# Scores of two heads at once on four quarters of TensorE, in two attention layers of a decoder kernel

## What is computed

```python
q_hk = (hidden_q @ Wq.T).reshape(Bv, Sv, H, K)
q_big = jnp.einsum('bshk,hkq->bshq', q_hk, w_kc_q)
q_big = _apply_rope(q_big, sin_q[None, :, None, :], cos_q[None, :, None, :])
kv_r = _apply_rope(kv_c, sin_k[None], cos_k[None])
q_r = jnp.einsum('bshq,hqr->bhsr', q_big, W_qr)
k_r = jnp.einsum('bld,hdr->bhlr', kv_r, W_kr)
scores = jnp.einsum('bhsr,bhlr->bhsl', q_r, k_r)
attn = jax.nn.softmax(scores, axis=-1)
ctx_c = jnp.einsum('bhsl,bld->bhsd', attn, kv_r)
ctx_lat = jnp.einsum('bhsd,hkd->bhsk', ctx_c, w_kc_kv)
```

## Time and profile before

| | us |
|---|---|
| runs, median (lowest, highest) | 1348.82 (1344.62, 1350.92) |
| profiled execution, its own time | 1344.42 |
| its span, first to last instruction | 1342.7 |
| TensorE busy in it | 1245.0 |
| VectorE busy | 798.1 |
| ScalarE busy | 591.1 |
| second layer's attention loop, first to last scores | 435.07 to 490.32 |
| third layer's attention loop, first to last scores | 829.69 to 961.60 |

### The profile page before, as it was taken

The page is one execution under the profiler, slowest core; times in us unless marked ns, Lnnn a source line. Parts: engine busy times, 40 slices in busy tenths (PEclk is TensorE's granted clock), DMA queues, the critical chain, the costliest instruction groups (busy, mean ns, idle before and its releaser), DMA issues. The chain is left out here.

```text
span 1342.7 us, 30256 instructions
## 1 busy us (share of the span) xinstructions
PE 1245.0 (93%) x12658; PEld 932.8 (69%) x12658; DVE 798.1 (59%) x1511; ACT 591.1 (44%) x1070; POOL 378.9 (28%) x323
## 2 busy tenths in 40 slices
PE   6999998989999999999999889999997888999988
PEld 3479994559977677788867667888774445676545
DVE  5764566863363764633358665888644775873762
ACT  3632334684554674433433431232532453662751
POOL 0164303046630000555520005544102043532100
PEclk9999999999999999999999999999998999999999
DMA  4000004046024001000075080000016421211000
GB/s 125 4 2 4 4 4 127 1 109 131 1 68 146 2 2 36 1 0 1 1 165 166 1 264 1 1 1 2 2 71 199 133 61 47 55 30 33 2 1 32
DMA packets 81047, 68.36 MB, mean 51 GB/s; under 512 B 24968, under 2 KB 76880, under 8 KB 80784
## 3 DMA queue, kind: packets, MB, share of 16 engines
q1 hardware_dynamic: 78096, 63.63, 16.8%
q0 software_dynamic: 768, 2.10, 0.5%
q10 hardware_dynamic: 2048, 0.70, 0.2%
HBM read 53.82 MB, written 8.39 MB: 46 GB/s over the span
## 5 line engine op out<-in xcount | busy, mean ns | idle before, releaser
L1955 PE MATMUL ps<-rounded 128*128 128x512 f32 x384 | 91.2, 393 | 2.0 <-POOL rounded L1988 1.0
L1688 PE MATMUL ps<-fixed 128*128 128x512 bf16 x361 | 89.6, 389 | 1.9 <-PEq L78 1.9
L1342 POOL TENSOR_TENSOR fixed<-fixed,cross 128x768 f32<-128x768 f32 x32 | 58.9, 1839 | 104.5 <-DVE cross L1291 104.5
L1955 PEld LDWEIGHTS ps<-rounded 128*128 128x128 f32 x384 | 70.9, 188 | 20.3 <-POOL rounded L1988 5.3
L1256 PE MATMUL ps<-rounded 128*128 128x256 f32 x576 | 76.8, 287 | 1.3 <-DVE cross L1287 1.3
L1256 PEld LDWEIGHTS ps<-rounded 128*128 128x128 f32 x576 | 70.7, 190 | 5.4 <-issue 3.2
L1988 POOL TENSOR_TENSOR rounded<-weights,rounded 128x256 fp32r<-128x256 f32 x32 | 23.6, 760 | 179.7 <-ACT rounded L2006 179.7
L1321 ACT COPY cross<-ps 128x256 f32<-128x256 f32 x32 | 11.9, 372 | 112.9 <-PE ps L1265 112.9
L1688 PEld LDWEIGHTS ps<-fixed 128*128 128x128 bf16 x361 | 34.7, 99 | 37.8 <-issue 6.9
L2095 DVE TENSOR_TENSOR work<-work,ps 128x512 f32<-128x512 f32 x32 | 22.0, 687 | 62.0 <-ACT work L2023 59.9
L1629 POOL TENSOR_TENSOR work<-weights,work 64x512 f32<-64x512 f32 x32 | 41.2, 1287 | 54.3 <-DMA work<-work 33.5
(11 more groups left out here) (497 smaller groups left out, 3056.0 us busy)
## 6 DMA issues: line engine op xcount, KB each, us to landing
weights<-in_L_ffn_masksT SPq DMA_DIRECT2D x32, 256.0 KB, 6.1
weights<-in_L_ffn_fc_w SPq DMA_DIRECT2D x16, 256.0 KB
weights<-in_L_xattn_Wq SPq DMA_DIRECT2D x2, 2048.0 KB, 10.1
weights<-in_L_xattn_WoT SPq DMA_DIRECT2D x2, 2048.0 KB, 11.1
work<-work SPq DMA_DIRECT2D x64, 64.0 KB, 2.0
sorted_in<-work SPq DMA_DIRECT2D x1, 3072.0 KB, 15.3
work<-sorted_in SPq DMA_DIRECT2D x12, 256.0 KB, 2.9
sorted_out<-work SPq DMA_DIRECT2D x12, 256.0 KB, 2.1
```

The costliest lines, as they stand in the source:

```text
L1342: nc.gpsimd.tensor_tensor(ro[:, v % 2, :, :], ro[:, v % 2, :, :], sn, ALU.add).then_inc(s["roped"], 1)
L1688: k.nc.tensor.matmul(k.ps[:, bank, :], k.ident16, k.causal, start=True, stop=True)
L1955: last = nc.tensor.matmul(ps[:, 2 * (n % 2) + i, :], a[:, q % 2, i, c, :], b[:, c, half * BANK:(half + 1) * BANK], start=c == 0 and part = ...
```

## The change

In both layers the scores of two heads are made together (`pair_scores`), in every second iteration: 32 matmuls that go round all four quarters, head e of the pair into bank 4 + e. They wait until both former heads' scores are subtracted. In the second layer head e takes the row half e, sequence b the column half b % 2. In the third layer the row half is b % 2 and the column half (b + e) % 2, so that a bank gets results from both row halves; `qb` is laid out anew for that, and the second head's probabilities have their partition halves exchanged, which `weigh` undoes in its access pattern.

In the third layer ("halved") also:
- `narrow` uses the quarters for the first two of its three parts (8 matmuls of 64 x 64 x 128, the zero blocks are left out) and two column halves for the third (4 matmuls of 128 x 64 x 128), into the first 128 columns of the banks 2 and 3.
- A turn goes to the upper 256 columns of banks 2 and 3 in place of a bank of its own; turns wait for the copy of the narrow product, narrow products for the copy of a turn.
- TensorE's order in an iteration becomes: project 2h, narrow 2h - 1, tiles 0 and 1 of project 2h + 1, turn, tile 2 of it, scores (of a pair, in every second iteration), narrow 2h, weigh.
- ScalarE does the hook "act_b" (copy of narrow 2h, rounding of weights) after the copy of the turned block.

VectorE's and GpSimd's programs are unchanged. The diff's core:

```diff
+        def pair_scores(h):
+            if h >= 2:
+                pe.wait_ge(s["centred"], h)
+            pe.wait_ge(s["q_ready"], q_hooks["ready"](h))
+            for b in range(BATCH):
+                tok, at = b * SEQ, (b // 2) * SEQ
+                for e in range(2):
+                    r0, to = quarters(e, b)
+                    last = nc.tensor.matmul(ps[to:to + 64, 4 + e, at:at + SEQ], q_of(h + e, b), t.kk[r0:r0 + 64, tok:tok + SEQ],
+                                            start=True, stop=True, tile_position=(r0, to))
+                    if b == BATCH - 1:
+                        last.then_inc(s["scored"], 1)
+
         def turn(h):
             pe.wait_ge(s["probs"], h + 1)
-            gap = 1 if turn_banks[0] == turn_banks[1] else 2
+            gap = 1 if halved or turn_banks[0] == turn_banks[1] else 2
             if h >= gap:
                 pe.wait_ge(s["copied"], h + 1 - gap)
+            if halved:
+                pe.wait_ge(s["q_ready"], min(2 * (h + lag + 2), 2 * NH))
             for jp in range(4):
-                last = nc.tensor.transpose(ps[:, turn_banks[h % 2], jp * P:(jp + 1) * P],
+                to = ps[:, 2 + jp // 2, D + jp % 2 * P:D + (jp % 2 + 1) * P] if halved else ps[:, turn_banks[h % 2], jp * P:(jp + 1) * P]
+                last = nc.tensor.transpose(to,
                                            t.pr[:, h % 3, 2 * jp:2 * jp + 2, :].rearrange("p a t -> p (a t)"), k.ident)
...
+            if halved and h < NH:
+                q_hooks["pe_b"](pe, h)
+                if h >= lag + 2:
+                    turn(h - lag - 2)
+                q_hooks["pe_c"](pe, h)
             if lag <= h < NH + lag:
-                scores(h - lag)
-            if h < NH:
+                if quarters is None:
+                    scores(h - lag)
+                elif (h - lag) % 2 == 0:
+                    pair_scores(h - lag)
+            if halved and h < NH:
+                q_hooks["pe_d"](pe, h)
+            if not halved and h < NH:
                 q_hooks.get("pe_b", none)(pe, h)
...
             if h < NH:
                 q_hooks["act"](act, h)
-                q_hooks.get("act_b", none)(act, h)
+                if not halved:
+                    q_hooks.get("act_b", none)(act, h)
...
         def narrow(pe, v):
             pe.wait_ge(s["roped"], v + 1)
             if v:
                 pe.wait_ge(s["q_ready"], v)
-            for a in range(3):
-                last = nc.tensor.matmul(ps[:, 2, 0:D], c1[:, v // 4, a, :], ro[:, v % 2, a, :], start=a == 0, stop=a == 2)
+            if v // 2 >= lag + 2:
+                pe.wait_ge(s["copied"], v // 2 - lag - 1)
+            def of_parity(rows, a, b):
+                return ro[rows, v % 2, a, :].rearrange("p (j b t) -> p j b t", b=2, t=SEQ)[:, :, b, :]
+
+            for a in range(2):
+                for e, own in enumerate(halves):
+                    for b, to in enumerate(halves):
+                        nc.tensor.matmul(ps[to, 2 + e, 0:P], c1[own, v // 4, a, own], of_parity(own, a, b), start=a == 0, stop=False,
+                                         tile_position=(64 * e, 64 * b))
+            for e, own in enumerate(halves):
+                for b, to in enumerate(halves):
+                    last = nc.tensor.matmul(ps[to, 2 + e, 0:P], c1[:, v // 4, 2, own], of_parity(slice(0, P), 2, b), start=False, stop=True,
+                                            tile_position=(0, 64 * b))
             last.then_inc(s["narrowed"], 1)
...
-               1.0, turn_banks=(3, 3), lag=3)
+               1.0, lag=lag, quarters=lambda e, b: (64 * (b % 2), 64 * ((b + e) % 2)), halved=True)
```

More of the change, by code:

```diff
@@ L652, in weigh @@
                     for b in range(2):
+                        weights = t.pT[rows, u % 2, :, jp, b * SEQ:(b + 1) * SEQ]
+                        if halved:
+                            part, heads, row = (list(e) for e in weights.ap)
+                            weights = bass.AP(tensor=weights.tensor, offset=weights.offset,
+                                              ap=[part, [heads[0] + SEQ - 2 * SEQ * b, 2], row])
                         last = nc.tensor.matmul(ps[64 * b:64 * b + 64, 6 + a, jp * P:(jp + 1) * P], t.kvt[rows, 2 * jp + b, :],
-                                                t.pT[rows, u % 2, :, jp, b * SEQ:(b + 1) * SEQ], start=True, stop=True,
-                                                tile_position=(64 * a, 64 * b))
+                                                weights, start=True, stop=True, tile_position=(64 * a, 64 * b))
             last.then_inc(s["pv"], 1)
@@ L692, in _ @@
                     outputs(j, units)
-            if lag + 2 <= h < NH + lag + 2:
+            if max(lag + 2, NH if halved else 0) <= h < NH + lag + 2:
                 turn(h - lag - 2)
@@ L745, in _ @@
                     act.wait_ge(s["pv"], g // 2 - 1)
-                nc.scalar.copy(t.pT[:, (g // 2) % 2, g % 2, :, :].rearrange("p a b -> p (a b)"), ps[:, turn_banks[g % 2], :]).then_inc(s["copied"], 1)
+                to = t.pT[:, (g // 2) % 2, g % 2, :, :]
+                if halved:
+                    nc.scalar.copy(to.rearrange("p (n m) b -> p n (m b)", n=2), ps[:, 2:4, D:2 * D]).then_inc(s["copied"], 1)
+                else:
+                    nc.scalar.copy(to.rearrange("p a b -> p (a b)"), ps[:, turn_banks[g % 2], :]).then_inc(s["copied"], 1)
+            if halved and h < NH:
+                q_hooks["act_b"](act, h)
             if lag <= h < NH + lag:
@@ L1230, in attend_L2 @@
     t.mx, t.sm, t.rs = more.take(2, NT), more.take(2, NT), more.take(2, NT)
-    qb = more.take(2, TOK)
+    qb = more.take(2, 2, TOK // 2)
     sn = more.take(3, D)
@@ L1243, in attend_L2, with project @@
     with k.stage("h_top", "h_rest", "w_top", "w_rest", "cosed", "sined", "roped", *CORE_SEMS) as (block, s):
-        def project(pe, v):
+        def project(pe, v, tiles=range(3)):
             u, part = divmod(v, 4)
[L1246 to L1250, removed]
-            for a in range(3):
+            if 0 in tiles:
+                if v < 2:
+                    hold(k, 7, 12 - 6 * v)
+                pe.wait_ge(s["w_rest"], u + 1)
+                if u == 0:
+                    pe.wait_ge(s["h_rest"], part + 1)
+            for a in tiles:
                 if v and a != 1:
@@ L1257, in project @@
                                                 start=c == 0 and n == 0, stop=c == KC - 1 and n == 2)
-            last.then_inc(s["q_proj"], 1)
+            if 2 in tiles:
+                last.then_inc(s["q_proj"], 1)
         def narrow(pe, v):
@@ L1320, in copy_q @@
                 act.wait_ge(s["scored"], 2 * u - 2)
-            nc.scalar.copy(qb[:, u % 2, part * D:(part + 1) * D], ps[:, 2, 0:D]).then_inc(s["q_ready"], 1)
+            nc.scalar.copy(qb[:, u % 2, :, part * P:(part + 1) * P], ps[:, 2:4, 0:P]).then_inc(s["q_ready"], 1)
         def act_q(act, h):
```

18 lines of the change are left out of this document (10 added, 8 removed).

## The result

| | before | after |
|---|---|---|
| runs, median (lowest, highest), us | 1347.1 (1344.0, 1352.2) | 1352.5 (1347.3, 1355.7) |
| runs | 17 | 17 |
| profiled execution, its own time | 1344.42 | 1355.11 |
| its span | 1342.7 | 1353.4 |

The ratio of the times is 1.0037, with a 95% interval of 1.0024 to 1.0050: 5.0 us slower (3.2 to 6.7), against +4.7 forecast, and inside the half per cent that the forecast called "within". The runs of before measured beside it lie 1.7 us under those shown earlier.

What follows compares the result with a forecast made beforehand. TensorE, 93% busy, was taken as the bound, with VectorE only 12% idle in the third layer. Second layer -7.1 and third +11.8 give +4.7: 1349.1 us profiled, 1353.5 as median (+0.35%); eight-in-ten range 1343 to 1364.

Steps and rivals of the forecast that it cites:

- Four quarters wide: Scores in both layers: a pair's 64 passes run on four quarters in 1.08 us, where two heads took 2.16.
- Rival B: Scores: 64-column passes not issued densely enough; at 32 ns each a pair takes 2.05 us, +18 us, 1367; chance 0.15.
- Rival B2: Third layer's scores: one bank cannot be written from two row halves at once; +11.5 us, 1360; chance 0.05.
- Second layer: Second layer's attention: TensorE's time per pair of heads falls from 8.00 to 6.92 us, in all -7.1 us.
- Narrow products: Third layer: the narrow product on quarters takes 1.1 to 1.4 us against 1.33 to 1.49, nothing gained or lost.
- Order: Third layer: later scores hold VectorE's maximum, and the second projection's cosines queued behind it; VectorE idle about 3.1 us.
- the ring: Third layer: chained distances between projections and VectorE's cosines over two heads, 21.8 us against 19.66.
- Rival A: Third layer gains as the second does, VectorE's idle time absorbing the late maximum; wins 6.5 us, 1335; chance 0.10.
- single steps of 5.47 and 2.93 us: Third layer: second projection's start to its cosines, 5.47 us in an iteration with scores, 2.93 without.
- Third layer, the sum: Third layer's attention: +8.6 in four full periods, +2.5 in the iterations before, +0.7 in the tail; together +11.8 us.
- the granted clock: Both stretches: clock taken as 1.00; forecast wrong if it falls with the new idle time; no size given.
- Shared banks: Third layer: waits between turns and narrow products for ScalarE's copies stay hidden; uncovered, up to 0.6 us in 13 iterations.

Runs made afterwards that it cites:

- e5: Kernel after with the third layer's pair scores issued twice, over the same results; 1360.2 us, ratio 1.0099 to before.
- e3: Kernel after with the third layer's pair scores ahead of the second projection again; 1333.5 us, ratio 0.9912 to before; second run 1335.8 us, 0.9921.
- e4: Kernel after with the third layer's old narrow products, turn bank and order, only its scores paired on four quarters; 1337.1 us, ratio 0.9922 to before.
- e2: Kernel after with the second layer's attention as before, so only the third layer changed; 1360.6 us, ratio 1.0102 to before.
- e7: Kernel after with the third layer's turn behind tile 2 of the second projection, ahead of the scores; 1351.4 us in one run.
- e8: e3 with the third layer's turn behind the whole second projection; 1334.5 us, ratio 0.9915 to before.
- e1: Kernel after with the third layer's attention as before, so only the second layer changed; 1338.6 us, ratio 0.9933 to before.
- e6: Kernel after with VectorE serving the third layer's second projection before it takes the maximum; 1353.3 us, ratio 1.0051 to before.

## Why the prediction was right, point by point

**Four quarters wide: right.** 1.08 us a pair was forecast, 1.09 came in the second layer. Rival B (32 or 25 ns a pass) needs 2.05 or 1.6 us: 64 passes in 1.09 us are 17 ns each, and e5's 15. The floor of about 25 ns from start to start that the Trainium skill states ("TensorE: Matmul & The Clock Gate", "Wait — 56ns, not 53.3ns?") doesn't hold across quarters in these runs. Rival B2 fell too. In the third layer, where a bank gets results from both row halves, the scores took 870.92 - 869.94 = 0.98 us with the narrow product behind them, and in e3, with a full product behind them as in the second layer, 896.08 - 894.99 = 1.09 us, the same as there. Asked for 869.940 to 869.960 alone, the timeline of after has four passes:

```profile
869.94 0.29 PE L642 MATMUL ps<-work,cross 64*64 64x64 f32 x4
```

Four passes have started within 20 ns, and the first four matmuls of the program take the four quarters, two of different row halves to a bank. (The trace doesn't name a pass's quarter; that these four are on the four quarters is read from the program.) The rule of the Trainium skill's "TensorEngine Tiling (Array Packing)" ("Gotcha 1: PSUM Pressure"), that different row tiles can't use one bank at the same time, is not borne out here either. The row L3026, with which the prediction argued, was weaker evidence: at 35 ns a pass it doesn't show two passes at once.

**Second layer: the sign and the places right, the size short by 1 us.** From the first scores to the last normalisation's start it took 60.31 us before (435.07 to 495.38), 52.10 after (434.80 to 486.90): -8.2, against -7.1 forecast. The term that was short is the period, 6.78 instead of 6.92. I took only the scores out of the sum; what surrounds them became 0.14 us cheaper as well: the product that begins behind the weighing 1.82 instead of 1.91, and a turn 0.44 instead of 0.49. That these are changes of tiling that dropped out is likely, since a pair has one visit of scores fewer, but only argued.

**Narrow products: right.** When stalled for GpSimd, one took 806.78 to the next projection at 808.10, 1.32 us; at the same places before it took 1.31 and 1.33 (807.60 to 808.91, 811.72 to 813.05). So 24 small passes on quarters cost what six of 256 columns do. No run shows a gain from them (e3 beside e4).

**Order: right, and it is the whole of the loss.** The idle piece ahead of the maximum was put at about 3.1 us and is 3.20; the ring at 21.8 and is 21.60; TensorE near 80% busy, and it is 80%. Rival A needed a maximum less than 1 us late. e3 takes that one cause away and the loss turns into a gain; e5 lengthens it and the period follows one to one; e2 shows it without the second layer. The ring's single steps of 5.47 and 2.93 us came out as 5.3 (867.19 to 872.49) and 2.9 (879.20 to 882.06, with 0.65 of that VectorE's idle time).

**Third layer, the sum: +14.15 measured in the profiled executions, +11.8 forecast.** By terms, with the last normalisation counted to its start (the prediction's 25.3 us before counts to its end, 966.65 + 0.69):

| stretch | before | after | forecast | measured |
|---|---|---|---|---|
| first projections, iterations 0 to 3 | 24.84 | 24.86 | 0 | 0.0 |
| iterations 3 to 7 | 38.11 | 41.68 | +2.5 | +3.6 |
| iterations 7 to 15 | 78.56 | 86.40 | +8.6 | +7.8 |
| iteration 15 to last normalisation | 24.57 | 27.30 | +0.7 | +2.7 |

The third term was 0.8 too large, because the ring came out at 21.60 and not 21.8. The two that were too small are the second and the last, and both have the same ground: the granted clock, which the prediction named as what would make it wrong, fell. In iterations 3 to 7 two projections took 2.98 and 3.53 us instead of 2.38; the second of them in the timeline, and the busy time by stretch behind its start:

```profile
852.33 3.53 PE L1296 MATMUL ps<-rounded 128*128 128x256 f32 x18 [2.05 <-DVE cross L1340]
```

```profile
853.10:856.50 3.40, 3.40 (x28) 3.18 (x28) 3.02 (x4) 0.00 (x0) 1.83 (x1) 0.50 0.00 0
```

That is 1.7 us in two projections, and the term is over by 1.1. The first of the two shows how much comes through: in e7, whose order is the same up to there and whose clock stayed up, the next iteration's projection begins 8.25 us after it (830.40 to 838.65), in after 9.15 (831.16 to 840.31). e5, whose clock stayed up behind both, settles the term: its iterations 3 to 7 take 42.38 us, and without its two extra rounds of scores of 0.94 each 40.50, which is +2.4 against before, where +2.5 was forecast. In the tail TensorE has its longest idle piece, and behind it everything up to 969 runs at half the clock, the last scores too:

```profile
963.34 1.13 PE L1313 MATMUL ps<-fixed,work 64*64 64x128 f32 x16 [3.78 <-POOL fixed L1395]
...
967.09 1.99 PE L642 MATMUL ps<-work,cross 64*64 64x64 f32 x64
```

```profile
955.80:962.30 6.50, 3.76 (x126) 3.04 (x124) 4.58 (x8) 2.68 (x5) 1.35 (x2) 1.00 0.01 3
962.30:969.10 6.80, 5.20 (x93) 4.05 (x93) 4.37 (x6) 2.22 (x5) 0.98 (x1) 0.50 0.01 4
```

The scores alone took 969.01 - 967.09 = 1.92 there instead of 1.09, the narrow product 2.2 or so instead of 1.3; together with the turn some 2 us, which is what the term lacks. VectorE stood idle for those scores, where the prediction had chained its own work alone:

```profile
969.13 0.69 DVE L820 TENSOR_REDUCE cross<-ps 128x8 f32<-128x512 f32 x1 [2.29 <-PE ps L642]
```

e3 and its second run put a price on it. They are one kernel, and from the first projection of iteration 15 to the last normalisation the clock fell in the first (behind 2.15 us idle) and stayed up in the second:

```profile
929.51:954.64 25.13, 21.76 (x336) 17.98 (x336) 21.20 (x35) 11.63 (x22) 5.48 (x3) 0.86 0.01 2
...
935.13:957.85 22.72, 19.26 (x340) 15.84 (x342) 21.06 (x35) 11.98 (x23) 5.48 (x3) 1.00 0.01 3
```

The clock costs 25.13 - 22.72 = 2.4 us there. I had chained VectorE's work and never asked what TensorE's 3.8 idle us would do to its speed.

**Shared banks: right.** No wait of TensorE in after's steady pair names ScalarE; e8 shows the price once the cover is gone.

**Sum.** -8.2 and +14.2 are +6.0 in the two profiled stretches, -9.0 and +13.7 by e1 and e2, +5.0 for the whole by the timed runs; -7.1 and +11.8 were forecast. Both terms were too small, by 1.1 and 2.4 us in the traces and by 1.9 each in the timed runs, with opposite signs, so that the sum is nearer than its parts: part of the hit is luck.

Of the 10.7 us between the two profiled executions 4.7 more lie outside the two stretches, 3.5 between the two layers and the rest ahead of and behind them. At the second layer's end after was 8.5 us ahead (last normalisation at 486.90 against 495.38), at the third layer's first projection only 5.0 (795.62 against 800.57), with nothing of the change between. What differs there is the clock. After has two short stretches at half the clock between the layers:

```profile
713.10:716.60 3.50, 3.50 (x34) 3.34 (x32) 3.29 (x5) 1.90 (x3) 0.00 (x0) 0.51 0.48 167
740.40:743.90 3.50, 3.34 (x22) 3.01 (x23) 2.71 (x4) 1.07 (x2) 0.00 (x0) 0.51 0.00 0
```

and before has one (710.60 to 714.00, at 0.50). From the second layer's last normalisation to the third's first projection the eleven profiled executions sort by the number of such stretches: with none (e3, e5, e6, e8) it takes 304.0 to 304.1 us, with one (before, e2) 305.2, with two (e1, e4, e7, after and the second run of e3) 307.3 to 308.7. The work between is the same in all of them, and one kernel, e3, stands in the first group and in the last (304.0 and 307.7). So these 3.5 of the 10.7 us are the clock's, and the kernels with the second layer's change lie on both sides of before. Why the clock falls there in one execution and not in the next is not shown.

## What to carry to other kernels

Before an engine's order is changed, read the order of the engine that consumes from it: an operation moved later costs its delay if the consumer meets it ahead of something that the next step needs, even where the producer has idle time to spare. Move the small operation that others are queued behind forward, not back. And where a change opens an idle piece on TensorE, of 3.8 us but also of 2, price what follows it at both clock levels.

## What the runs showed of the hardware that was not expected

- **The clock after short idle pieces.** The same piece, 2.05 us without work ahead of a projection, stands twice in after, in e2, in e5 and in e7. In after the clock fell to half behind both, in e2 behind the first (that projection takes 3.79 us, the second 2.38); in e5 and e7 it stayed at 1.00 behind all four, with nearly the same work before (TensorE busy for 2.1 to 2.3 of the 4.1 to 4.3 us up to the projection in after, e5 and e7). Busy time by stretch ahead of the first piece's end and behind it, after and then e7:

```profile
826.90:831.10 4.20, 2.21 (x89) 1.77 (x88) 2.90 (x5) 1.92 (x3) 0.44 (x1) 1.00 0.01 2
...
832.60:836.00 3.40, 3.40 (x32) 2.70 (x31) 1.79 (x3) 0.00 (x0) 1.29 (x1) 0.51 0.03 5
```

```profile
826.20:830.40 4.20, 2.15 (x90) 1.77 (x89) 2.96 (x5) 1.98 (x3) 0.39 (x1) 1.00 0.01 2
830.40:836.00 5.60, 5.12 (x54) 4.53 (x55) 3.81 (x7) 0.68 (x2) 2.41 (x2) 1.00 0.02 3
```

  The length of the piece alone doesn't decide it. Behind 3.8 us (the tails of after, e2, e5 and e7) and 2.62 us (e6, all five) the clock fell each time, in e2's tail only 1.2 us after work had begun again. Behind 2.15 us it fell in the tail of e3 and stayed up in the tail of the same kernel's second run. In e6 it fell once behind a piece of 1.32 us (954.15) and stayed up behind one of 1.31 (848.86). What decides stays open; no run was made for it.
- **Passes on four quarters.** 15 to 17 ns from one to the next with 64 columns each, half of what two quarters gave (33.8), with the same rate whether a bank is written from one row half or from both (1.09 us for 64 passes with a full product behind them, in the second layer and in e3's third).
